# A two-layer decoder on one core: TensorE's order in the hybrid attention loop, ScalarE's copies there, and filler products in the head

## The chip, the core and the metric

The kernel runs on one core of a Trainium2 chip. A core has five engines that take their instructions in order and wait for each other on semaphores: TensorE (PE) multiplies matrices out of the on-chip memory into eight banks of result memory (`PS[:, 0..7, :]`), VectorE (DVE) and ScalarE (ACT) read and write both memories, GpSimd (POOL) works on the on-chip memory alone, and SyncE (SP) starts transfers. The metric is the device time of the whole program in microseconds (us), the median of three runs.

## What is computed

Eight sequences of 256 tokens with 256 features pass through six residual blocks, each on the layer-normalised state. Cut to what matters:

```python
x = x + mixer(ln(x))                       # low-rank state mixer, folded into one 256x256 matrix
x = x + cross_attention(ln(x), ctx, mask)  # one head, 64 context tokens, masked
x = x + bit_ffn(ln(x))                     # ternary weights, activations rounded to 8 bits, biases
x = x + self_attention(ln(x))              # 16 heads of 16, causal
x = x + hybrid_attention(ln(x), ctx)       # 16 query heads, 4 key heads of 128, RMS norm and rotary
                                           # turn on queries and keys; keys are 64 context tokens
                                           # plus the causal 256 tokens
x = x + top1_experts(ln(x))                # router of 32 experts, masked ternary weights

def hybrid(x, ctx):                        # the block that most of the change is in
    q = rope(rms(x @ wq) * qw); k = rope(rms(x @ wk) * kw); k_ctx = rms(ctx @ wk_ctx) * kw
    p = softmax(q @ concat(k_ctx, k).T / sqrt(128) + causal)
    return (p @ concat(ctx @ wv_ctx, x @ wv)) @ wo
```

## The kernel before

The stages follow each other: a head (mixer and cross attention of all batches, and the rounding of the feed-forward weights) up to about 82 us of the profiled span, the feed-forward block to about 190 us, self attention to about 435 us, the hybrid block from there to about 1093 us, and the routed experts. Every engine has its own program, written out by hand, and the order in it is the order on the chip.

**The hybrid loop** (`hybrid` in each engine's program) runs over 8 batches; batches 0 to 2 are written out, 3 to 6 come from a loop over pairs, and 7 is written out. Each batch has 8 iterations i, one for each half of the tokens (j = i // 4) and each key head (g = i % 4) with its 4 query heads. u = 8b + i counts them. One iteration works on several u at once. TensorE, in order:

- `scores(u+1, (0, 1))`: two of the four score tiles, into banks 3 and 4, out of `eQT`, the turned query;
- one odd piece of work (`values`, `xt_turn`, `keys`, `route`, `turn_keys`), which with few exceptions writes bank 2;
- `raw_query(u+3)`: four 512-wide passes into bank 1;
- `outputs(u-2)`: the turned probabilities `ePT` times the values, into bank 0;
- more odd pieces (`values(b, par, 1)` at i = 0, `keys` 0 and 1 at i = 1 and 2), `hybrid_out` (32 passes with `wo`, bank 2) at i = 4 for the batch before and at i = 7 for this one;
- `scores(u+1, (2, 3))`;
- `turn_query(u+2)`: the finished query `eQA` is turned into bank 2;
- `turn_probs(u-1)`: 5 turned tiles for the first half of the tokens (j = 0), 9 for the second, into banks 5, 6 and 7.

ScalarE copies bank 2 to `eQT` (`turned_query`, L1682), takes the squares of the raw query (`query_squares`, L1675), the exponentials (`exps`, L1691), the full turned tiles of bank 5 (`turned_probs`, L1698) and the output (`outputs`, L1705), and empties bank 2 for the odd pieces (`raw_keys` L1617 and L1618, `turned_keys` L1626 to L1631, `values` L1711 to L1714). VectorE masks scores and takes their maxima (`masked_max`, L847), turns the query by its angle (`rotate_query`, L817 and L823) and finishes it (`finish_query`, L829 and L833), normalises (L856, L859), and copies the rest of the turned tiles (`turned_probs`, L866 to L868; L866 is the full tile in bank 6, for j = 1 only). For the next batch's keys it has `square_key` (L734) and `turn_key` (L745 to L759). At i = 7 come `token_stats` (L881, L885), `choose` (L906 to L917) and `hybrid_finish` (L873), which adds the block's output to the tokens and frees bank 2. GpSimd computes the scales (`query_scales`, `key_squares`, `key_scales`).

What sets the order at one place is a single line on TensorE: `scores(u+1, ...)` begins with `pe.wait_ge(e_qc, v + 1)`, ScalarE's copy of the turned query, and between `turn_query` and that wait only `turn_probs` stands.

**The head** (`head(n)`, n = 0 to 8) does mixer work for batch n+1 and cross attention for batch n. On ScalarE six calls of `magnitude` (L1502) sum the weights, which then gives the scale `rgam`; `rounding` (L1508) rounds six pieces; VectorE clips them and makes the rows of biases (`bias_rows`, L460 to L467: a chain of eight instructions at n = 4). All matrix helpers go through `product` at L1842, so TensorE's rows carry that line; tiles tell them apart: `wq` is `raw_query`, `arena` into `EW`, `w_in` or `w_out` is `outputs`, `wk` is `keys`, `EW` with `arena` is `scores`.

## Time and profile before

| | us |
|---|---|
| median of 3 runs | 1186.63 (1184.10 to 1187.51) |
| the profiled execution | 1187.17 |
| its span in the trace | 1184.3 |
| TensorE busy | 1041.7 (88%) |
| VectorE busy | 877.1 (74%) |
| ScalarE busy | 653.8 (55%) |
| GpSimd busy | 326.3 (28%) |

TensorE's busy time counts a modelled end for each pass, so short waits are partly hidden in it; the distance from one start to the next is the safer reading. Its granted clock has two levels, 2.4 GHz (1.00 in the rows) and 1.2 GHz. In a timeline, "x4" joins four passes (two 32-bit products), and the bracket gives idle time before the first one with what ended it.

### The profile page before, as it was taken

Reading aid. Unit: us, or ns where it says so; the run is one execution under the profiler, and the core shown is the slowest. Engines: PE = TensorE matmul, PEld = TensorE weight load, DVE = VectorE, ACT = ScalarE, POOL = GpSimd, SP = SyncE. Lnnn points to the kernel's source line nnn. Section 1 sums busy time; section 2 is a strip of 40 time slices with the busy share of each in tenths; the row PEclk is TensorE's granted clock in tenths of the full one; section 3 lists DMA queues with packets and bytes.
Section 4 is the critical chain, followed back from the end, with each engine's and each line's share of the span. In section 5 each row is a group of like instructions: output and inputs, shape, how many; then the busy total and the mean of one; then the engine's idle time right before and its main releaser. Section 6 shows DMA issues by size and latency. Waiting matters only on the chain.

```text
span 1184.3 us, 21508 instructions
## 1 busy us (share of the span) xinstructions
PE 1041.7 (88%) x6293; PEld 716.7 (61%) x6301; DVE 877.1 (74%) x2458; ACT 653.8 (55%) x2010; POOL 326.3 (28%) x528
## 2 busy tenths in 40 slices
PE   7788886898999957899999999999999999988395
PEld 5654445676666634565766756657666666666385
DVE  5777774778877767877877878878878788764285
ACT  2777783655555524556556565565565645741262
POOL 3342222111111321312323223223232232101465
PEclk7979997999999978899999999999999999999598
DMA  9710001111111004000000000000000000000731
GB/s 286 251 35 2 1 1 54 55 55 54 53 53 53 19 1 133 26 1 14 1 14 1 1 14 1 5 10 1 16 1 0 14 1 0 15 1 24 263 99 45
DMA packets 38875, 49.58 MB, mean 42 GB/s; under 512 B 5110, under 2 KB 29564, under 8 KB 38528
## 3 DMA queue, kind: packets, MB, share of 16 engines
q1 hardware_dynamic: 36160, 44.16, 12.4%
q0 software_dynamic: 2304, 4.24, 1.0%
q8 instruction: 35, 0.57, 0.2%
q14 instruction: 56, 0.46, 0.1%
q10 hardware_dynamic: 320, 0.15, 0.1%
HBM read 32.70 MB, written 14.78 MB: 40 GB/s over the span
## 4 chain that ended last, share of the span: by engine, by line
PE 47%; ACT 4%; issue 4%; POOL 4%; DVE 3%; DMA 0%; DVEq 0%; ACTq 0%; POOLq 0%
PE PS L1842 41%; POOL out_dram L1417 3%; PE PS L2229 2%; PE PS L2209 2%; ACT arena L1682 1%; POOL tokens_dram L1393 1%; PE PS L2086 1%; DVE arena L823 1%; ACT arena L1691 1%; DVE arena L859 0%; DVE arena L847 0%; ACT early L1618 0%; PE PS L2231 0%; PE PS L2274 0%; PE PS L1852 0%
## 5 line engine op out<-in xcount | busy, mean ns | idle before, releaser
L1842 PE MATMUL PS<-early,arena 128*32 128x128 f32 (+6 forms) x920 | 122.2, 361 | 46.0 <-DVE early L713 23.7
L1842 PE MATMUL PS<-EW,arena 128*128 128x256 f32 (+7 forms) x512 | 121.2, 360 | 16.8 <-DVE small L847 7.3
L1842 PE MATMUL PS<-wq,EW 128*128 128x512 f32 x256 | 125.7, 614 | 6.8 <-DVE arena L823 6.6
L1331 POOL TENSOR_SCALAR small<-small 128x4 f32<-128x4 f32 x64 | 18.6, 291 | 385.2 <-ACT mask L1675 215.5
L1842 PEld LDWEIGHTS PS<-early,arena 128*32 128x32 f32 (+4 forms) x928 | 62.4, 121 | 99.8 <-issue 38.0
L847 DVE CUSTOM_DVE_ANT_0 arena<-PS,kmask 128x128 f32<-128x128 f32 (+3 forms) x256 | 91.4, 389 | 41.4 <-PE PS L1842 35.9
L1691 ACT ACTIVATE arena<-arena,small 128x128 f32<-128x128 f32 (+3 forms) x256 | 119.5, 473 | 0.5 <-DVE small L852 0.3
L1842 PE MATMUL PS<-wo,early 128*128 128x256 f32 x512 | 115.0, 384 | 3.6 <-DVE sinT L900 2.8
L1842 PEld LDWEIGHTS PS<-EW,arena 128*128 128x128 f32 x512 | 83.5, 193 | 43.7 <-issue 23.0
L1842 PEld LDWEIGHTS PS<-wo,early 128*128 128x128 f32 x512 | 98.6, 193 | 17.7 <-DVE sinT L900 3.2
L1682 ACT ACTIVATE arena<-PS 128x512 f32<-128x512 f32 x64 | 38.2, 597 | 114.5 <-PE PS L2209 114.1
L781 DVE TENSOR_REDUCE small<-PS 128x4 f32<-128x512 f32 x64 | 58.2, 951 | 43.1 <-PE PS L1842 43.1
L1675 ACT ACTIVATE mask<-PS 128x128 f32<-128x128 f32 x256 | 66.6, 275 | 41.0 <-PE PS L1842 40.8
L1842 PEld LDWEIGHTS PS<-wq,EW 128*128 128x128 f32 x256 | 45.4, 192 | 50.4 <-issue 42.2
L1333 POOL TENSOR_TENSOR small<-small,halves 128x4 f32<-128x4 f32 x64 | 69.1, 1079 | 5.4
L859 DVE TENSOR_SCALAR arena<-arena,small 128x128 f32<-128x128 f32 (+3 forms) x256 | 68.8, 333 | 2.3
L1611 ACT ACTIVATE early<-PS 128x384 f32<-128x384 f32 x64 | 28.6, 488 | 72.3 <-PE PS L2113 72.2
L1842 PE MATMUL PS<-arena,EW 128*128 128x512 f32 (+1 forms) x160 | 63.4, 510 | 2.6 <-ACT arena L1698 2.1
L1656 ACT ACTIVATE arena<-PS,small 128x256 f32<-128x256 f32 x128 | 63.1, 493 | 0.0
L1655 ACT ACTIVATE arena<-PS,small 128x128 f32<-128x128 f32 x128 | 48.8, 381 | 25.1 <-DVE small L781 24.5
L1217 POOL TENSOR_SCALAR ve<-mv 128x2 f32<-128x2 f32 x23 | 5.1, 223 | 190.9 <-DVE mv L416 190.3
L2113 PE MATMUL PS<-ident,arena 128*128 128x128 f32 x384 | 55.5, 279 | 0.4 <-ACT early L1611 0.4
(343 smaller groups left out, 2435.7 us busy)
## 6 DMA issues: line engine op xcount, KB each, us to landing
EW<-in_masksT_dram SPq DMA_DIRECT2D x32, 256.0 KB, 3.5
tokens_dram<-EW SPq DMA_DIRECT2D x1, 4160.0 KB, 16.1
arena<-tokens_dram SPq DMA_DIRECT2D x16, 260.0 KB, 2.8
results_dram<-EW SPq DMA_DIRECT2D x32, 128.0 KB, 3.2
EW<-results_dram SPq DMA_DIRECT2D x4, 1024.0 KB, 10.5
X<-in_x_dram SPq DMA_DIRECT2D x8, 256.0 KB, 5.1
wq<-in_wq_dram SPq DMA_DIRECT2D x1, 2048.0 KB, 11.1
wo<-in_wo_dram SPq DMA_DIRECT2D x1, 2048.0 KB, 18.5
```

Of the source, the lines that this page charges most:

```text
L781: last = dve.tensor_reduce(d_neg[:, i % 2, j, :], PS[:, 0:4, at:at + n], AX.X, ALU.max, negate=True)
L847: dve.tensor_tensor_reduce(probs(i, t), PS[:, 3 + t % 2, 0:n], kmask[:, at:at + n], 1.0, LOWEST, ALU.add, ALU.max, e_max[:, t:t + 1]).then ...
L859: last = dve.tensor_scalar(probs(i, t), probs(i, t), e_inv[:, t:t + 1], None, ALU.mult)
L1333: pool.tensor_tensor(e_rqs[:, i % 2, :], e_q3[:, i % 2, :], halves[:, 0:GH], ALU.pow).then_inc(e_rq, 1)
L1417: pool.indirect_dma_start(out_rows[:, :], bass.IndirectOffsetOnAxis(ap=to, axis=0), sY[:, k, t, :], None, bounds_check=B * S - 1, oob_is_e ...
L1655: act.activation(dP[:, i % 2, r, 0:P], PS[:, r, 0:P], ACT.Exp, bias=d_neg[:, i % 2, 0, r:r + 1])
L1656: act.activation(dP[:, i % 2, r, P:3 * P], PS[:, r, P:3 * P], ACT.Exp, bias=d_neg[:, i % 2, 1, r:r + 1]).then_inc(d_e, 1)
L1675: last = act.activation(eSQ[:, h * XD:(h + 1) * XD], PS[:, 1, h * XD:(h + 1) * XD], ACT.Square, accum_out=e_q2[:, i % 2, h:h + 1])
L1682: act.activation(eQT.rearrange("p (t h q) -> p h t q", t=4, h=GH), PS[:, 2, :].rearrange("p (h t q) -> p h t q", t=4, h=GH), ACT.Copy).the ...
L1691: last = act.activation(tile, tile, ACT.Exp, bias=e_neg[:, i % 2, t:t + 1], accum_out=e_sum[:, i % 2, t:t + 1])
L1842: return pe.matmul(dst, lhs, rhs, start=first, stop=last)
L2113: last = pe.transpose(PS[:, 4 + r % 2, k * P:(k + 1) * P], dP[:, i % 2, r, k * P:(k + 1) * P], ident[:, :])
```

## The change

In the **hybrid loop**, TensorE: `turn_query(u+2)` now stands ahead of `outputs(u-2)`. `keys` 0, 1 and 2 are made at i = 1, 3 and 4, ahead of `raw_query` (before: 0 and 1 at i = 1 and 2, behind `outputs`, and 2 at i = 3). `values(b, par, 1)` goes to bank 7 instead of bank 2. `hybrid_out` stands ahead of `outputs` too. ScalarE: `exps` moves ahead of the evictions of bank 2, `turned_query` ahead of `outputs`, and `turned_probs` also copies bank 6 where j = 1, which VectorE's L866 did. VectorE's `square_key` moves from i = 2, 3, 4 to i = 2, 4, 7, and GpSimd's key work follows the new times.

In the **head**: of the bias rows' chain, four of the scalings and copies move to ScalarE (`bias_round`, at n = 4, 5, 6; biasB's last scaling among them) and two combining steps stay on VectorE, spread over n = 5 and 6. `rounding` is spread, one piece at a time, over the starts and ends of n = 4 to 7. `cross_normalise` stands ahead of the computation of `gam`. TensorE gets `keep_going`: products of ones whose result nobody reads, 8 ahead of the wait for `c_fold`, 3 ahead of `folds`, 4 at each n from 4 to 8 (10 at n = 7), and twice 4 in `head_end`.

```diff
+            def bias_round(k):
+                act.wait_ge(s_c, mark["unit"] if k == 0 else mark[f"rest{k - 1}"])
...
@@ ScalarE, hybrid
-            def turned_probs(v):
+            def turned_probs(v, i):
                 act.wait_ge(e_t, v + 1)
                 after(act, e_pv, v)
-                act.activation(ePT[:, 0:512], PS[:, 5, :], ACT.Copy).then_inc(e_pta, 1)
+                for k in range(1 + i // XG):
+                    last = act.activation(ePT[:, 512 * k:512 * k + 512], PS[:, 5 + k, :], ACT.Copy)
+                last.then_inc(e_pta, 1)
...
-                        turned_probs(u - 2)
+                        turned_probs(u - 2, (i - 2) % 8)
+                    exps(u, i)
...
-                    exps(u, i)
                     if further[3]:
                         query_squares(u + 3, (i + 3) % 8)
+                    if i == 0:
+                        values(b, par, 1)
                     if i == 7 and routed:
                         weights(b - 2)
+                    if further[2]:
+                        turned_query(u + 2)
                     if i >= 2:
                         outputs(b, i - 2)
@@ VectorE, hybrid
-                if i >= XG:
-                    dve.tensor_copy(ePT[:, 512:1024], PS[:, 6, :])
...
-                    if 2 <= i <= 4 and nxt[0] == HYBRID:
-                        square_key(nxt[1], i - 2)
+                    if i in (2, 4, 7) and nxt[0] == HYBRID:
+                        square_key(nxt[1], {2: 0, 4: 1, 7: 2}[i])
@@ TensorE, head and hybrid
+            def keep_going(n, at=6):
+                for _ in range(n):
+                    product(PS[:, at, 0:P], ones[:, :], ones[:, :])
...
+                if n >= 4:
+                    keep_going(10 if n == B - 1 else 4, 4)
...
-                    if i == 3 and more:
-                        keys(nxt[1], 1 - par, 2)
+                    if i in (1, 3, 4) and more:
+                        keys(nxt[1], 1 - par, {1: 0, 3: 1, 4: 2}[i])
...
                         raw_query(u + 3, (i + 3) % 8, pars[3])
-                    if i >= 2:
-                        outputs(u - 2, i - 2, par)
...
                     if i == 0:
-                        pe.wait_ge(e_vr, 2 * b + 1)
-                        values(b, par, 1)
+                        after(pe, e_ptd, u - 1)
+                        values(b, par, 1, 7)
...
                         turn_query(u + 2, (i + 2) % 8)
+                    if i >= 2:
+                        outputs(u - 2, i - 2, par)
```

TensorE's order at i = 3 of a batch in the loop over pairs, before (`wk` is `keys`, `wq` the raw query, `arena` into `w_in` and `EW` the outputs, `EW` into `arena` the scores, L2209 the turn of the query, L2229 the turned probabilities):

```order
L1842 MATMUL PS<-wk,EW 128x512 x2
L283 REGISTER_ALU
L1842 MATMUL PS<-wq,EW 128x512 x2
L1842 MATMUL PS<-arena,w_in 128x512
L1842 MATMUL PS<-arena,EW 128x256
L283 REGISTER_ALU
L1842 MATMUL PS<-EW,arena 128x288
L283 REGISTER_ALU
L1842 MATMUL PS<-EW,arena 128x320
L2353 REGISTER_ALU
L2209 MATMUL PS<-ident,arena 128x128 x4
L2229 MATMUL PS<-ident,arena 128x128 x4
```

and in the change (L2231 and L2251 are the same two turns):

```order
L1854 MATMUL PS<-wk,EW 128x512 x2
L283 REGISTER_ALU
L1854 MATMUL PS<-wq,EW 128x512 x2
L283 REGISTER_ALU
L1854 MATMUL PS<-EW,arena 128x288
L283 REGISTER_ALU
L1854 MATMUL PS<-EW,arena 128x320
L2361 REGISTER_ALU
L2231 MATMUL PS<-ident,arena 128x128 x4
L1854 MATMUL PS<-arena,w_in 128x512
L1854 MATMUL PS<-arena,EW 128x256
```

The outputs moved from in front of the scores to a place behind the turn of the query.

TensorE's order at i = 7, before (`wo` is `hybrid_out`):

```order
L1842 MATMUL PS<-wq,EW 128x512 x2
L1842 MATMUL PS<-arena,EW 128x512 x2
L1842 MATMUL PS<-arena,w_out 128x256
L1842 MATMUL PS<-wo,early 128x256 x16
L283 REGISTER_ALU
L1842 MATMUL PS<-EW,arena 128x160
L283 REGISTER_ALU
L1842 MATMUL PS<-EW,arena 128x192
L2209 MATMUL PS<-ident,arena 128x128 x4
L2229 MATMUL PS<-ident,arena 128x128 x8
L2231 MATMUL PS<-ident,arena 128x128
```

and in the change:

```order
L1854 MATMUL PS<-wq,EW 128x512 x2
L1854 MATMUL PS<-wo,early 128x256 x16
L283 REGISTER_ALU
L1854 MATMUL PS<-EW,arena 128x160
L283 REGISTER_ALU
L1854 MATMUL PS<-EW,arena 128x192
L2231 MATMUL PS<-ident,arena 128x128 x4
L1854 MATMUL PS<-arena,EW 128x512 x2
L1854 MATMUL PS<-arena,w_out 128x256
L2251 MATMUL PS<-ident,arena 128x128 x8
L2253 MATMUL PS<-ident,arena 128x128
```

`hybrid_out` follows the raw query at once, and the outputs follow the turn of the query.

ScalarE's order at i = 6, before (L1698 turned probabilities, L1626 to L1631 turned keys, L1691 exponentials, L1675 squares):

```order
L1698 ACTIVATE arena<-PS 128x512
L1626 ACTIVATE EW<-PS 128x4x128
L1628 ACTIVATE EW<-PS 128x4x64
L1631 ACTIVATE EW<-PS 128x4x128
L1691 ACTIVATE arena,small<-arena,small 128x256 x2
L1691 ACTIVATE arena,small<-arena,small 128x320 x2
L1671 REGISTER_ALU
L1675 ACTIVATE mask,small<-PS 128x128 x4
```

and in the change (L1713 turned probabilities, L1705 exponentials, L1640 to L1645 turned keys, L1689 squares):

```order
L1713 ACTIVATE arena<-PS 128x512 x2
L1705 ACTIVATE arena,small<-arena,small 128x256 x2
L1705 ACTIVATE arena,small<-arena,small 128x320 x2
L1640 ACTIVATE EW<-PS 128x4x128
L1642 ACTIVATE EW<-PS 128x4x64
L1645 ACTIVATE EW<-PS 128x4x128
L1685 REGISTER_ALU
L1689 ACTIVATE mask,small<-PS 128x128 x4
```

The exponentials moved ahead of the turned keys, and there are two copies of turned tiles instead of one.

## Rows read from the trace of the kernel before

**Rows 1.** Busy us of PE, PEld, DVE, ACT, POOL over 50 us; clock; DMA; GB/s

```profile
750.00:800.00 50.00, 48.32 (x207) 30.86 (x205) 38.26 (x134) 29.70 (x113) 11.91 (x23) 1.00 0.04 9
```

**Rows 2.** TensorE's timeline, one hybrid batch: start us, us, engine, line, operation, [idle before]

```profile
751.26 1.98 PE L1842 MATMUL PS<-wq,EW 128*128 128x512 f32 x4 [0.46 <-DVE arena L823]
...
755.23 7.07 PE L1842 MATMUL PS<-wo,early 128*128 128x256 f32 x32
...
781.64 0.86 PE L1842 MATMUL PS<-EW,arena 128*128 128x160 f32 x4
783.01 0.66 PE L2209 MATMUL PS<-ident,arena 128*128 128x128 f32 x4 [0.50 <-ACT early L1618]
...
785.49 1.88 PE L1842 MATMUL PS<-wq,EW 128*128 128x512 f32 x4
787.21 1.02 PE L1842 MATMUL PS<-arena,w_in 128*128 128x512 f32 x2
...
788.50 1.88 PE L1842 MATMUL PS<-wk,EW 128*128 128x512 f32 x4
...
790.65 0.76 PE L1842 MATMUL PS<-EW,arena 128*128 128x160 f32 x4
791.25 0.60 PE L2209 MATMUL PS<-ident,arena 128*128 128x128 f32 x4
...
792.13 0.27 PE L2231 MATMUL PS<-ident,arena 128*128 128x128 f32 x1
792.70 1.07 PE L1842 MATMUL PS<-EW,arena 128*128 128x224 f32 x4 [0.30 <-ACT arena L1682]
...
829.64 0.71 PE L1842 MATMUL PS<-EW,arena 128*128 128x96 f32 x4
830.80 1.55 PE L1842 MATMUL PS<-wq,EW 128*128 128x512 f32 x3 [0.46 <-DVE arena L823]
```

**Rows 3.** ScalarE's timeline in the same batch

```profile
791.97 0.60 ACT L1682 ACTIVATE arena<-PS 128x512 f32<-128x512 f32 x1 [0.88 <-PE PS L2209]
...
823.50 0.60 ACT L1626 ACTIVATE EW<-PS 128x512 f32<-128x512 f32 x1 [0.77 <-PE PS L2086]
...
824.74 0.52 ACT L1691 ACTIVATE arena<-arena,small 128x256 f32<-128x256 f32 x1
...
826.81 0.27 ACT L1675 ACTIVATE mask<-PS 128x128 f32<-128x128 f32 x1
```

**Rows 4.** VectorE's timeline in the same batch

```profile
755.41 0.69 DVE L747 TENSOR_TENSOR early<-early,cosk 128x512 f32<-128x512 f32 x1
...
762.45 0.42 DVE L873 TENSOR_TENSOR X<-X,PS 128x256 f32 x1 [1.66 <-PE PS L1842]
...
822.95 0.68 DVE L866 COPY arena<-PS 128x512 f32<-128x512 f32 x1
...
825.57 0.69 DVE L833 TENSOR_TENSOR arena<-arena,small 128x512 f32<-128x512 f32 x1
```

**Rows 5.** TensorE's timeline, first batch of the hybrid loop

```profile
496.49 1.94 PE L1842 MATMUL PS<-EW,arena 128*128 128x224 f32 x4 [3.76 <-DVE small L847]
...
498.97 3.78 PE L1842 MATMUL PS<-wq,EW 128*128 128x512 f32 x4
```

**Rows 6.** TensorE's timeline in the head

```profile
13.92 3.75 PE L1842 MATMUL PS<-early,arena 128*128 128x256 f32 x8 [0.78 <-DVE early L534]
```

**Rows 7.** VectorE's timeline in the head

```profile
51.59 0.48 DVE L462 TENSOR_SCALAR early<-early,small 128x512 f32<-128x512 f32 x1
...
55.12 0.69 DVE L541 TENSOR_TENSOR X<-X,PS 128x512 f32<-128x512 f32 x1
```

**Rows 8.** ScalarE's timeline in the head

```profile
25.88 1.05 ACT L1502 ACTIVATE arena<-EW 128x1024 f32<-128x1024 f32 x1
```

**Rows 9.** SyncE's transfers, first 60 us: issue of the third weight

```profile
10.46 0.60 SPq L1132 DMA_DIRECT2D EW<-in_outT_dram  x1
```

**Rows 10.** Transfers by line, first 60 us: KB each, median us to landing

```profile
EW<-in_outT_dram SPq DMA_DIRECT2D x1, 1024.0 KB, 14.9
```

125 lines of the change are left out of this document (65 added, 60 removed).

## The prediction

> **What bounds the kernel now.** I first read the busy times of 50 us stretches: from 500 to 1050 us, the hybrid loop, TensorE is busy about 97% at full clock, VectorE 77% and ScalarE 59% [rows 1]. So there only what TensorE does not spend on its own passes can be won. I then read its timeline from start to start. One batch lasts 830.80 - 751.26 = 79.54 us [rows 2]. Its passes back to back: a raw query 787.21 - 785.49 = 1.72, outputs 788.50 - 787.21 = 1.29 for j = 0 and, with two more 512-wide passes, 2.15 for j = 1; second pair of scores 791.25 - 790.65 = 0.60 for j = 0, and by its columns 1.02 for j = 1; `hybrid_out`, 32 passes, 7.07 less the usual 0.17 of overlap = 6.90 [rows 2]. Summed: 8 raw queries 13.8, outputs 13.8, 3 `keys` and 2 `values` 8.7, `hybrid_out` twice 13.8, scores 12.3 (the first pairs at 0.54 and 0.91), query turns 3.5, probability turns 6.1 (0.55 and 0.98), the other turns and routing 2.9: 74.9 us. So **4.6 us of a batch are waits**, and that is the most that the reordering can return per batch.
>
> Where they are [rows 2]: after the last turned tile at 792.13, the scores start at 792.70; 0.11 of the 0.57 is the tile itself, 0.46 a wait for ScalarE's copy of the turned query. It comes where only 5 tiles are turned in between (i = 1 to 4), so 1.84 a batch. At 781.64 to 783.01 the scores take 1.37 instead of 0.60: 0.77 for the eviction of the context keys. At 829.64 to 830.80 the raw query waits 0.6 for VectorE. The other 1.4 are pieces under 0.35.
>
> **The hybrid part, step by step.** A turned query needs from the turn's start 791.25 to ScalarE's start at 791.97 [rows 3] 0.72, then 0.60 and 0.13 until scores start: 1.45 (792.70 - 791.25). Now outputs and turned tiles lie in between: 0.44 + 1.29 + 0.55 = 2.28 in the shortest iteration. The 1.84 goes, with 0.8 to spare if ScalarE is there in time. It is: its squares take 1.0 and begin when the raw query ends, 0.6 + 0.72 before the copy is due.
>
> `keys` ahead of `raw_query` give the eviction 1.72 + 0.60 of cover, so the 0.77 goes, although `exps` (826.81 - 824.74 = 2.07 for j = 1, 1.65 for j = 0) [rows 3] now stand before it: counted from the iteration's start, at i = 1 ScalarE ends its token norm at 0.9, two copies at 2.0, `exps` 3.6, `raw_keys` 4.6; TensorE asks at 0.54 + 1.86 + 1.72 + 0.60 = 4.7. Cover is exactly used up. At i = 2 the turned input is evicted at 3.2 to 3.3, asked for at 3.3. `values(b, par, 1)` in bank 7 drops one wait of 0.25.
>
> VectorE loses a 0.68 copy four times a batch [rows 4], and its rotation of the query no longer waits behind scores that come after outputs. The wait at 830.80 goes.
>
> **Waits that the change makes.** At i = 6 ScalarE has, from the start: two copies to 1.15, `exps` to 3.2, three copies of turned keys 824.74 - 823.50 = 1.24 [rows 3] to 4.45; TensorE is ready to write bank 2 after 0.91 + 0.43 + 1.72 + 1.02 = 4.1. Wait **0.5**. At i = 7 `hybrid_out` begins 2.15 + 0.6 earlier, but what frees bank 2 is `hybrid_finish`, at the end of VectorE's queue. Before, VectorE's L747 to the end of `choose` ran from 755.41 to 762.45 - 1.66 = 760.79, and it was 1.66 early [rows 4]. After: `exps` end at 3.2 of the iteration, normalising 4.65, `square_key` (new here, 0.6) 5.25, the 5.4 us block 10.65, `hybrid_finish` 11.1. TensorE asks at 0.54 + 1.72 + 6.90 + 0.60 = 9.76. Wait **1.4**. With 0.1 elsewhere the new waits are 2.0, so a batch gains 4.6 - 2.0 = **2.6**, and the new period is 76.9.
>
> By batch: 2 to 6 gain 5 x 2.6 = 13.0. Batch 1 routes nothing, `choose` is missing and the 1.4 with most of its cause: 3.8. Batch 0 has no `outputs` to cover VectorE's key turns at i = 4; TensorE idled 3.76 there and then ran a raw query at half clock, 3.78 against 1.88 [rows 2, 5]. `square_key` moved away, and the scores come earlier, but VectorE's chain (four copies and masks, 2.0; query 1.4; normalising after `exps` at 4.7; then 0.6, 1.3 and 2.7) ends at 9.3 where TensorE asks at 7.65: 1.7 to 2.1 idle remain. With the waits of its other iterations, 6.5; with the clock kept, 9; without, 4. Batch 7 has no next batch; its routing now waits behind `exps`: 1.0 (-1 to 3). **Hybrid: 24.3.**
>
> A rule of the Trainium skill speaks against the copies' move: "ScalarE: Activation LUTs", section "Rules for kernel authors", wants plain elementwise work on VectorE and budgets about 0.3 us plus 0.83 ns per element for an ACTIVATE, an estimate of 0.72 for 512. Here the copy lasts 0.60 on ScalarE and 0.68 on VectorE [rows 3, 4], so the trace disagrees. By the page the wait at i = 6 would grow from 0.5 to 0.9 and the sum shrink by some 3 us.
>
> **The head.** The mixer's 8 passes at 13.92 take 3.75 at half clock [rows 6]; at full clock they would take about 1.9. The 8 fillers fit before `c_fold` and could save 1.8 here and 1.0 just before. But ScalarE's first `magnitude` starts at 25.88 [rows 8] and needs the third weight, issued at 10.46 and 14.9 under way [rows 9, 10]: landed at 25.4. So no more than about 0.5 passes that point on ScalarE; what TensorE gains in being early may add 1. At n = 4 VectorE's bias chain, 55.12 - 51.59 = 3.53 [rows 7], holds the next mixer's addition; it goes, and 1.5 comes back at n = 5 and 6. ScalarE gets four passes of 0.5 and is next in the chain, so I take 1.5 of it. Fillers after n = 4 cost 34 x 0.21 = 7 us of TensorE at full clock if they were all on the path, less what a kept clock returns. Bounds -5 to +7; I take **3.0**, nearest to the bias chain less the ScalarE work. The feed-forward and self-attention stages and the tail are untouched.
>
> **Sum:** 24.3 + 3.0 = 27.3 off the profiled 1187.17: 1159.9. The median lies 0.5 below that execution, but the terms are no finer: **1160**.
>
> **Rivals.** (a) *ScalarE late.* It now begins each iteration behind a copy of outputs that come last on TensorE. The cover at i = 1, 2, 5, 6 was 0 to 0.8; if each copy comes 0.6 later than I have it, four waits of 0.6 take 2.4 of the 2.6, and 7 batches give back 16: 1176. For it: the zeros of cover above. Against: ScalarE is idle 0.88 before the copy at 791.97 [rows 3].
>
> (b) *VectorE late: slower.* `finish_query` had 3.3 us of slack behind outputs; now the turn of the query asks 3.3 after the start at i = 2 and 4.1 at i = 5, 6. Before, from the copy at 822.95 to the multiply's end at 826.26 were 3.3 [rows 4], 2.7 without the copy. That decides: if the rotation ends more than 0.6 after the iteration's start, as it did in this row (1.0), each such iteration waits. With 1.25 at i = 2, 3, 5, 6, a batch pays 5.0 + 2.0 against 4.6, +2.4, and 7 batches +17; without the head's gain 1203. Against: squares end 1.2 and rotation 2.6 after the raw query, the next iteration starts after 2.9.
>
> (c) *The head pays.* Fillers stand in the path at half clock: +6, so 1169.
>
> (d) *Nearly all waits go.* The block at i = 7 is shorter than I count and batch 0 keeps its clock: 2 us more in six batches, 2.5 in batch 0, 3 in the head: 1146.
>
> **Chances.** Forecast (1153 to 1167) 0.50; (a) or part of it, 1167 to 1181, 0.20; (c) 0.08; (d) 0.12; (b) 0.06; no gain because (a) and (c) join, 0.04. The range 1148 to 1178 leaves out (b), half of (d) and the ends of (a). Measurement tells 0.3%, 3.6 us, from nothing: faster 0.90, same 0.04, slower 0.06.
>
> **What would show it.** Right: a batch period of 77 us; no wait of the scores on the turned query's copy; a turn of the query that waits about 1.4 for VectorE's addition at i = 7 and about 0.5 for ScalarE's turned keys at i = 6; about 2 us idle at i = 4 of batch 0; the first 82 us shorter by about 3. Wrong: waits of the query's turn on VectorE's multiply at i = 2, 5 or 6 (b), or a head that ends later than before.

## The result, and the profile after

The changed kernel takes 1175.87 us, median of 5 runs (1173.85 to 1176.54); beside it the kernel before takes 1186.58 us, median of 5 (1182.61 to 1187.51). The ratio is 0.9915, with a 95% interval of 0.9894 to 0.9935: faster, by 10.7 us. The forecast was 27 us, so the sign and the range held and the size did not. Three later comparisons, each on one chip, gave ratios of 0.9899, 0.9895 and 0.9905.

The profiled execution after has a span of 1174.1 us (before: 1184.3). The difference of 10.2 us is split up in one table, read off TensorE's timeline: the moments at which the `values` product of each batch begins, and VectorE's last `hybrid_finish`.

| us | before | after | gain | forecast |
|---|---|---|---|---|
| start of the first `values` product (end of head, feed-forward and self-attention) | 453.19 | 453.34 | -0.2 | 3.0 |
| batch 0 | 75.51 | 70.03 | 5.5 | 6.5 |
| batch 1 | 78.10 | 74.51 | 3.6 | 3.8 |
| batches 2 to 6, each | 78.68 to 79.78 | 77.33 to 77.56 | 9.4 in all | 13.0 |
| batch 7, to the start of the last `hybrid_finish` | 89.27 | 96.06 | **-6.8** | 1.0 |
| from there to the end | 91.5 | 92.8 | -1.3 | 0 |

The middle of the loop is what was foreseen. Busy time of PE, PEld, DVE, ACT and POOL in the stretch of [rows 1], with clock, DMA share and GB/s: TensorE went from 48.32 to 49.97 of 50 us. The stretch lies between two of the new waits, so it looks better than the batch as a whole.

```profile
750.00:800.00 50.00, 49.97 (x225) 33.33 (x224) 37.88 (x127) 31.28 (x115) 13.17 (x19) 1.00 0.04 9
```

TensorE's timeline of the same batch after the change, to be held against [rows 2] (start us, us, engine, line, operation, idle before):

```profile
784.19 0.27 PE L2253 MATMUL PS<-ident,arena 128*128 128x128 f32 x1
784.29 0.98 PE L1854 MATMUL PS<-EW,arena 128*128 128x224 f32 x4
...
811.12 0.66 PE L2231 MATMUL PS<-ident,arena 128*128 128x128 f32 x4 [0.48 <-ACT EW L1645]
...
823.82 0.76 PE L1854 MATMUL PS<-EW,arena 128*128 128x160 f32 x4
826.16 0.66 PE L2231 MATMUL PS<-ident,arena 128*128 128x128 f32 x4 [1.58 <-DVE X L870]
```

The scores at 784.29 start 0.10 after the turned tile at 784.19; before, they came 0.57 after it. The waits on the turned query and on the keys are gone. Two new ones stand where they were expected: 0.48 for ScalarE's turned keys at iteration 6, and at iteration 7 the scores take 2.34 us to the next start (826.16 - 823.82) instead of 0.60, so 1.74 go to waiting for VectorE's addition in `hybrid_finish` (L870).

The surprise is the last batch. TensorE's timeline at iterations 6 and 7, first in the kernel before, then in the changed one:

```profile
1054.75 0.60 PE L2274 MATMUL PS<-ident,causal 128*128 128x128 f32 x4
1055.19 1.88 PE L1842 MATMUL PS<-arena,EW 128*128 128x512 f32 x4
...
1057.34 0.97 PE L1842 MATMUL PS<-rwT,XT 128*128 128x32 f32 x8
...
1066.29 8.85 PE L1842 MATMUL PS<-wo,early 128*128 128x256 f32 x32 [2.78 <-DVE sinT L900]
```

```profile
1036.96 1.08 PE L1854 MATMUL PS<-rwT,XT 128*128 128x32 f32 x8 [2.79 <-ACT XT L1745]
...
1038.98 3.53 PE L1854 MATMUL PS<-arena,EW 128*128 128x512 f32 x4
...
1050.33 10.02 PE L1854 MATMUL PS<-wo,early 128*128 128x256 f32 x32 [6.36 <-DVE sinT L897]
```

Before, after turning the tokens (L2274) TensorE ran `outputs` and came to `route` (the `rwT` product) when ScalarE had copied the turned tokens. After, it waits 2.79 us for that copy (L1745), and the `outputs` that follow run at half clock (3.53 instead of 1.88). Then, ahead of `hybrid_out`, it waits 6.36 us for VectorE's copy of the logits (L897) instead of 2.78, and the output product takes 10.02 us instead of 8.85 (6.9 is its length at full clock). ScalarE's timeline says why `route` is late:

```profile
1034.26 0.51 ACT L1705 ACTIVATE arena<-arena,small 128x256 f32<-128x256 f32 x1
...
1036.33 0.58 ACT L1745 ACTIVATE XT<-PS 128x512 f32<-128x512 f32 x1
```

The copy stands behind the 2.07 us of `exps` (L1705), which the change put ahead of it.

### The profile page after: what moved, and what is told of

Its sections match the earlier page's. It is cut to its first block, busy times and chain, and to the rows that moved or that the text cites. A ratio compares the mean times of both kernels' runs of the same rounds, so it can differ in the third digit from the quotient of the medians.

```text
span 1174.1 us, 21695 instructions
## 1 busy us (share of the span) xinstructions
PE 1032.6 (88%) x6383; PEld 719.0 (61%) x6383; DVE 850.6 (72%) x2422; ACT 669.1 (57%) x2046; POOL 319.8 (27%) x528
## 4 chain that ended last, share of the span: by engine, by line
PE 40%; issue 6%; ACT 5%; POOL 4%; DVE 2%; SPq 1%; DMA 0%; DVEq 0%; POOLq 0%; ACTq 0%
PE PS L1854 33%; PE PS L2251 3%; POOL out_dram L1415 3%; PE PS L2231 3%; ACT arena L1705 2%; ACT arena L1713 1%; POOL small L1323 1%; PE PS L2253 1%; PE PS L2108 1%; SPq L1189 1%; DVE small L878 0%; ACT mask L1689 0%; ACT EW L1645 0%; ACT EW L1640 0%; DVE X L870 0%
## 5 line engine op out<-in xcount | busy, mean ns | idle before, releaser
L1854 PE MATMUL PS<-early,arena 128*32 128x256 f32 (+6 forms) x928 | 118.2, 353 | 45.5 <-DVE early L712 23.7
L1854 PE MATMUL PS<-EW,arena 128*128 128x256 f32 (+7 forms) x512 | 115.6, 349 | 11.3 <-DVE small L846 8.4
L1854 PE MATMUL PS<-wq,EW 128*128 128x512 f32 x256 | 123.2, 604 | 1.5 <-DVE arena L822 1.5
L1705 ACT ACTIVATE arena<-arena,small 128x128 f32<-128x128 f32 (+3 forms) x256 | 119.5, 475 | 4.1 <-DVE small L851 4.1
L1854 PEld LDWEIGHTS PS<-early,arena 128*32 128x32 f32 (+4 forms) x928 | 59.6, 118 | 98.0 <-issue 34.5
L1689 ACT ACTIVATE mask<-PS 128x128 f32<-128x128 f32 x256 | 67.1, 281 | 47.6 <-PE PS L1854 47.3
L1696 ACT ACTIVATE arena<-PS 128x512 f32<-128x512 f32 x64 | 38.9, 608 | 85.4 <-PE PS L2231 85.4
L1721 ACT ACTIVATE early<-PS 128x512 f32<-128x512 f32 x64 | 38.2, 597 | 84.7 <-PE PS L1854 84.7
L1713 ACT ACTIVATE arena<-PS 128x512 f32<-128x512 f32 x96 | 53.9, 596 | 13.9 <-PE PS L2253 11.7
```

Of the source, the lines that this page charges most:

```text
L1689: last = act.activation(eSQ[:, h * XD:(h + 1) * XD], PS[:, 1, h * XD:(h + 1) * XD], ACT.Square, accum_out=e_q2[:, i % 2, h:h + 1])
L1696: act.activation(eQT.rearrange("p (t h q) -> p h t q", t=4, h=GH), PS[:, 2, :].rearrange("p (h t q) -> p h t q", t=4, h=GH), ACT.Copy).the ...
L1705: last = act.activation(tile, tile, ACT.Exp, bias=e_neg[:, i % 2, t:t + 1], accum_out=e_sum[:, i % 2, t:t + 1])
L1713: last = act.activation(ePT[:, 512 * k:512 * k + 512], PS[:, 5 + k, :], ACT.Copy)
L1721: act.activation(eOT[:, GH * g:GH * g + GH, j * P:(j + 1) * P].rearrange("p h (t q) -> p h t q", t=4), PS[:, 0, :].rearrange("p (t h q) -> ...
L1854: return pe.matmul(dst, lhs, rhs, start=first, stop=last)
```

## The experiments

All kernels are named by what differs from the changed kernel. Times are compared within one group, since groups ran on different chips (the kernel before had medians of 1184.8 to 1188.9 us there). The changed kernel itself ran again in three of the five groups. It did not run in that of the token copy, the two outputs, the addition and the first run of the old head; there the ratio to the kernel before is the measure (0.9895 to 0.9915 for the changed kernel elsewhere). The stage durations of all profiles stand in the table at the end of this section.

**The last batch: the token copy ahead of the exps.** ScalarE, `hybrid`:

```diff
                     if i >= 2 or former:
                         turned_probs(u - 2, (i - 2) % 8)
+                    if i == 6 and not more:
+                        token_copy(b - 1, 2)
                     exps(u, i)
...
-                    if i == 6 and not more:
-                        token_copy(b - 1, 2)
```

> The changed kernel with one thing put back: in the last cross-attention batch, at iteration 6, ScalarE copies the turned tokens (token_copy) ahead of the exps of that iteration, as in the kernel before. The span of the changed kernel lost 6.8 us between the first values product and the last hybrid_finish of the last batch (96.06 us against 89.27 before). Theory 1 (this one copy behind the exps delays route, the logits and the output product, and lets the clock fall): the wait of 2.79 us ahead of route falls below 1, the wait of 6.36 us ahead of the last output product falls to about 3, the last batch comes to 91 or less, and the time is 3 to 6 us under the 1175.9 of the changed kernel: about 1171. Rival (the other moves in that batch, ScalarE's two copies of turned probabilities or the outputs behind the long output product, hold it): the last batch stays above 94, the time is within 1.5 us of 1175.9.

Measured 1166.99 us (ratio to before 0.9852, 0.9818 to 0.9887). The last batch took 92.5 us. TensorE's timeline:

```profile
1031.32 1.08 PE L1854 MATMUL PS<-rwT,XT 128*128 128x32 f32 x8 [0.74 <-ACT XT L1745]
...
1033.34 1.88 PE L1854 MATMUL PS<-arena,EW 128*128 128x512 f32 x4
...
1042.99 10.21 PE L1854 MATMUL PS<-wo,early 128*128 128x256 f32 x32 [6.36 <-DVE sinT L897]
```

The wait for `route` falls from 2.79 to 0.74 and the outputs behind it run at full clock (1.88). But the wait of 6.36 has not moved at all: half of the theory falls. The copied logits (L897) come behind VectorE's `normalise` and `choose` of iteration 7, and these behind the exps and the turned probabilities of that iteration, which follow TensorE's own turns (L2253). That chain is as long as before. What changed is what TensorE does meanwhile.

**And the two outputs ahead of the output product.** As above, with TensorE's order in the last two iterations of the last batch put back:

```diff
+                    if i >= 6 and not more:
+                        outputs(u - 2, i - 2, par)
                     if i == 6 and not more:
                         route(b - 1, 2)
...
-                    if i >= 2:
+                    if 2 <= i < (8 if more else 6):
                         outputs(u - 2, i - 2, par)
-                    elif former:
+                    elif i < 2 and former:
```

> As last_copy, and in iterations 6 and 7 of the last batch TensorE's outputs stand ahead of route and of the long output product, as in the kernel before. Theory 1 (the copy alone holds the loss): within 1 us of last_copy, about 1171. Rival (the output product ahead of the two outputs holds the other half, since the outputs ran while TensorE would have waited for the logits): 2 to 4 us below last_copy, 1168 to 1169, and the last batch at 88 to 89 us.

Measured 1167.04 us (0.9838, 0.9808 to 0.9869), the same median as with the copy alone; the last batch took 90.1 us.

```profile
1043.32 0.59 PE L1854 MATMUL PS<-arena,w_out 128*128 128x256 f32 x2
1046.68 8.86 PE L1854 MATMUL PS<-wo,early 128*128 128x256 f32 x32 [2.77 <-DVE sinT L897]
```

Now the outputs fill the chain: 2.77 us of waiting are left, as before the change (2.78), and the output product takes 8.86 us instead of 10.21, also as before the change (8.85). The last batch in twelve profiles of unchanged code there lies between 93.6 and 97.7 us, mean 95.6. So the copy alone (92.5) is 1.1 below the lowest of them, and both together (90.1) 3.6 below, within 0.8 of the kernel before. So these two moves hold the loss, 6.8 us in the first pair of profiles. How it divides between them is known only roughly: by stage durations 3 and 2.4, from one profile each, while the medians of the two kernels are equal; the start of the loop scatters by more than the second.

**VectorE's addition ahead of the token statistics.**

```diff
                         if nxt[0] == HYBRID:
                             turn_key(nxt[1], 2)
+                        if nxt[0] == HYBRID:
+                            hybrid_finish(b, 0)
                         if former and nxt[0] == HYBRID:
                             token_stats(b - 1)
                         if routed:
                             choose(b - 2)
                         if nxt[0] == HYBRID:
-                            hybrid_finish(b, 0)
                             if routed:
```

> The changed kernel with one thing moved: at iteration 7 of every batch but the last, VectorE's hybrid_finish (eight rows of the output product into the residual) stands ahead of token_stats and choose instead of behind them. The trace shows TensorE waiting 1.6 to 1.7 us per batch there, ahead of turning the query. Theory 2 (that wait is real and nothing takes its place): 1.4 to 1.7 us for each of 7 batches, 10 to 12 us off: 1164 to 1166. Rival (normalise and rotate of the next iterations are late instead, so that ScalarE's or VectorE's chain gives the wait back at the next scores): less than 4 us off, 1172 or more.

Measured 1165.85 us (0.9828, 0.9797 to 0.9860). The steady period falls from 77.5 to 75.8 us: 1.4 to 1.7 for each batch from 2 to 6, and 0 and 0.1 for batches 0 and 1, which pay no such wait. VectorE's and TensorE's timelines at the end of iteration 7:

```profile
819.64 0.42 DVE L870 TENSOR_TENSOR X<-X,PS 128x256 f32 x1 [0.81 <-PE PS L1855]
```

```profile
819.44 0.76 PE L1855 MATMUL PS<-EW,arena 128*128 128x160 f32 x4
820.12 0.66 PE L2232 MATMUL PS<-ident,arena 128*128 128x128 f32 x4
```

VectorE now waits for TensorE (0.81) and TensorE no longer for VectorE: the turn of the query follows the scores in 0.68. The wait was real, and nothing took its place. That the time is the expected one is in part luck: the 10 to 12 us off counted seven batches; five pay the wait, and their stage durations give 7.9.

**ScalarE's turned keys ahead of its exps at iteration 6.**

```diff
+                    if i == 6 and more:
+                        turned_keys(nxt[1], 1 - par, 1)
                     exps(u, i)
...
-                    if i == 6 and more:
-                        turned_keys(nxt[1], 1 - par, 1)
```

> The changed kernel with one thing moved: at iteration 6 of every batch but the last, ScalarE's copy of the turned keys stands ahead of the exps instead of behind. TensorE waits 0.48 us there per batch. Theory (the wait is all that the order costs): it goes, 0.3 to 0.5 us a batch, 2 to 4 us in all, about 1173. Rival (the exps are then late, since the copy waits for TensorE to turn the keys, and the wait of the turned probabilities grows by as much or more): no gain, 1175 to 1179.

Measured 1169.92 us against 1172.35 of the changed kernel in that group (ratios 0.9877 and 0.9899, their intervals overlap); the period falls from 77.5 to 76.8. The 0.48 goes, a wait of 0.58 for VectorE's rotation comes in iteration 7, and the wait for the addition shrinks to 0.77, since TensorE arrives later at it. So one delay was moved and one merged:

```profile
814.60 1.98 PE L1854 MATMUL PS<-wq,EW 128*128 128x512 f32 x4 [0.58 <-DVE arena L822]
...
824.86 0.66 PE L2231 MATMUL PS<-ident,arena 128*128 128x128 f32 x4 [0.77 <-DVE X L870]
```

**The second full tile of turned probabilities on VectorE again.** This undoes one part of the change:

```diff
                 after(dve, e_pv, v)
+                if i >= XG:
+                    dve.tensor_copy(ePT[:, 512:1024], PS[:, 6, :])
...
-                for k in range(1 + i // XG):
-                    last = act.activation(ePT[:, 512 * k:512 * k + 512], PS[:, 5 + k, :], ACT.Copy)
-                last.then_inc(e_pta, 1)
+                act.activation(ePT[:, 0:512], PS[:, 5, :], ACT.Copy).then_inc(e_pta, 1)
```

> The changed kernel with one thing put back: VectorE again copies the second full tile of turned probabilities in iterations 4 to 7 (0.68 us each) instead of ScalarE (0.60). Theory (VectorE is the later engine at iterations 4 and 7, ScalarE only at 6): 0.5 to 1.5 us a batch slower, 1179 to 1186, since hybrid_finish and the masked maxima come later by 0.68. Rival (ScalarE is the later engine in most of the batch, and the copy that it took over costs more than it brings): 1170 to 1175.

Measured 1167.26 us (0.9856, 0.9824 to 0.9888) against 1172.35 (0.9899, 0.9871 to 0.9927). The intervals just overlap; the durations of the batches decide. The rival holds in its sign, the theory doesn't, and the time is below the range of both. The period is 76.5 instead of 77.5 us, without the wait at iteration 6 and with 1.15 instead of 1.6 to 1.7 at iteration 7:

```profile
815.92 0.76 PE L1854 MATMUL PS<-EW,arena 128*128 128x160 f32 x4
817.82 0.66 PE L2231 MATMUL PS<-ident,arena 128*128 128x128 f32 x4 [1.15 <-DVE X L872]
```

Although VectorE has 0.68 us more to do in that iteration, it ends sooner: its `normalise` waits for the exps, and these stood behind ScalarE's second copy. Both engines must be done before TensorE goes on, but in this order: ScalarE, then VectorE. Work moved from the second of a chain to the first lengthens the chain unless the second was busy in the meantime; here VectorE was waiting (0.71 us ahead of L855 in the changed kernel):

```profile
818.13 0.18 DVE L855 RECIPROCAL small<-small 128x4 f32<-128x4 f32 x1 [0.71 <-ACT arena L1705]
...
825.69 0.42 DVE L870 TENSOR_TENSOR X<-X,PS 128x256 f32 x1
```

The Trainium skill ("ScalarE: Activation LUTs", section "Rules for kernel authors") gives plain elementwise work to VectorE. For this copy the run agrees with its advice, though not with the reason, VectorE's speed per element: one copy lasts 0.60 us on ScalarE and 0.68 on VectorE, and the gain comes from which of the two is waited for. The budget that the prediction takes from the same section is for an ACTIVATE with its bias as a pointer operand, which this copy has not; the rows have 0.60.

**The first batch: masked maxima ahead of the turned keys.**

```diff
+                    if i == 4 and not former:
+                        masked_max(u + 1, (i + 1) % 8, (2, 3))
+                        rotate_query(u + 3, (i + 3) % 8)
                     if i == 4:
                         if nxt[0] == HYBRID:
                             turn_key(nxt[1], 0)
```

> The changed kernel with one thing moved: in the first cross-attention batch, at iteration 4, VectorE's masked_max of the later two heads and rotate stand ahead of the two turn_key of the next batch. The trace shows TensorE idle for 4.20 us there, ahead of the query product, and that product then at half clock (2.56 us instead of 1.88). Theory (those two masked maxima behind 14 key copies hold the whole idle): the idle falls below 1 us, the clock stays, the first batch's period falls from 74.5 to 69.5 to 71 and the time by 3.5 to 5. Rival (the turned keys come late for iteration 5 instead): the idle moves there, the period falls by less than 1.5 us.

Measured 1172.81 us against 1172.35 (0.9884 and 0.9899): no difference that the runs can tell. The first batch takes 68.2 us; in the eleven profiles of kernels that leave it as it is, 70.0 to 71.8. So 1.8 to 3.6 are gained there, less than expected, and the idle of 4.20 splits into 0.96, 1.39 and 0.41 instead of going. First the changed kernel, then this one:

```profile
492.80 1.81 PE L1854 MATMUL PS<-EW,arena 128*128 128x224 f32 x4 [4.20 <-DVE small L846]
...
495.15 2.56 PE L1854 MATMUL PS<-wq,EW 128*128 128x512 f32 x4
```

```profile
493.69 0.43 PE L2111 MATMUL PS<-ident,early 64*128 64x64 f32 x4 [0.96 <-issue]
494.05 1.98 PE L1857 MATMUL PS<-wq,EW 128*128 128x512 f32 x4
497.43 1.26 PE L1857 MATMUL PS<-EW,arena 128*128 128x288 f32 x4 [1.39 <-DVE small L846]
```

VectorE's own timeline tells why the idle was so long. Before the change, then after it, at the last step of turning the second key:

```profile
495.24 0.69 DVE L759 TENSOR_TENSOR early<-early,small 128x512 f32<-128x512 f32 x1
```

```profile
485.13 0.68 DVE L733 TENSOR_REDUCE small<-early 128x4 f32<-128x512 f32 x1
...
491.55 0.69 DVE L758 TENSOR_TENSOR early<-early,small 128x512 f32<-128x512 f32 x1 [2.43 <-POOL small L1323]
```

Before, VectorE went straight on. In the changed kernel it stands idle for 2.43 us, waiting for GpSimd's scale of that key: the change moved the key's sum of squares (`square_key`, here L733) from i = 3 to i = 4, directly ahead of the step that needs the scale, and GpSimd does its other work first. With the masked maxima and the rotation put in front, VectorE has that time filled. In the later batches the same wait of 2.4 to 2.7 us stands in VectorE's timeline, but TensorE has `hybrid_out` to do meanwhile. That the 2.43 is what lengthens TensorE's idle follows from the two timelines; no run moved `square_key` back.

**The head.** The changed loop with the head of the kernel before (no filler products, the bias rounded on VectorE):

> Head of the kernel before with the cross-attention part of the change. By the two traces the head gained nothing (the loop's first scores at 452.36 us against 452.20). Theory (the head is worth 0): 1175.5 to 1176.5, as the changed kernel. Rival (the head change did bring its 3 us and something in the first batch gives them back): 1178 to 1180. Rival (the fillers cost clock or time): 1172 to 1174.

> The head of the kernel before with the cross-attention part of the change, beside the changed kernel on the same chip. Theory (new head worth 1 to 3 us on the median): 1 to 3 above after_third. Rival (worth nothing): within 1 us.

> The head of the kernel before with the cross-attention part of the change, the measure for the next: about 2.5 us above after_fourth, one batch of about 79 us, ScalarE idle about 4 us ahead of the copies of turned probabilities at the start of batch 5.

This kernel ran in three groups: 1175.99 (ratio 0.9921), 1179.92 (0.9935; the changed kernel beside it 1177.40, 0.9895) and 1177.70 (0.9927; beside it 1175.29, 0.9905). So it looked as if the new head brought 2.4 to 2.5 us, though its profiles showed no earlier start of the loop. But all three of its profiles have one batch, number 5, of 79.1 to 79.6 us, where the changed kernel has 77.6. Batch 5 is the first after the loop over pairs of batches branches back. ScalarE's timeline there, and TensorE's:

```profile
835.99 1.08 ACT L1698 ACTIVATE arena<-PS 128x512 f32<-128x512 f32 x2 [4.50 <-issue]
```

```profile
839.84 0.66 PE L2206 MATMUL PS<-ident,arena 128*128 128x128 f32 x4 [1.81 <-ACT EW L1713]
```

ScalarE stands for 4.50 us with nothing that it waits for ("issue"), and TensorE then waits 1.81 for it. In the changed kernel the same gap is 2.1 to 2.2 and is hidden. Hence a kernel that puts only six one-column copies, of no use, at the start of ScalarE's program, so that its loop lies where it lies in the changed kernel:

```diff
             act.activation(h_table, ones[:, 0:1], ACT.Exp)
+            for k in range(509, 512):
+                act.activation(small[0:64, k:k + 1], ones[0:64, 0:1], ACT.Copy)
+                act.activation(small[64:128, k:k + 1], ones[64:128, 0:1], ACT.Copy)
```

> As hybrid_third, with six more one-column copies on ScalarE at the program's start (into columns that nothing reads, while its first inputs are still under way), so that its instructions of the loop stand at the places that they have in the changed kernel. Theory (at the loop's branch back ScalarE waits for its instructions, and how long depends on where they lie): its idle time there falls from 4.0 to 4.4 to 2.1 to 2.3, that batch from 79.1 or more to 77.6, and the time by 1.5 to 2. Rival (something that the old head leaves behind, or another engine's instructions, make it late): as hybrid_third within 1 us, with the 4 us idle.

Measured 1174.52 us (0.9902), batch 5 at 77.58 us, and the gap:

```profile
832.12 1.09 ACT L1701 ACTIVATE arena<-PS 128x512 f32<-128x512 f32 x2 [2.21 <-issue]
```

Six instructions more, 3.2 us less on the median (the intervals overlap), and 2.0 less in this one batch of the profile, where the three profiles without them agree. With that accident taken out, the old head (1174.5) is as fast as the new one (1175.3). The fillers alone:

```diff
-            keep_going(8)
...
-                if n >= 4:
-                    keep_going(10 if n == B - 1 else 4, 4)
...
-                keep_going(4, 4)
                 level_turn(0)
-                keep_going(4, 4)
...
-            keep_going(3)
```

> The changed kernel without the filler products of its head (the ten of the kernel before stay). Theory (they raise the clock between 55 and 80 us from 0.72 to 0.84 up to 0.86 to 0.93, but the chain through ScalarE's and VectorE's copies sets the end there): within 1 us of after_fourth. Rival (they are what the new head brings): 2 to 4 us slower than after_fourth. Rival (they stand in the path): 1 to 3 us faster.

Measured 1172.22 us (0.9887, 0.9855 to 0.9918) against 1175.29 (0.9905, 0.9873 to 0.9937): not slower, perhaps 3 us faster. Busy times and clock of two stretches of the head, first the kernel before, then the changed one, then the changed one without fillers:

```profile
0.00:55.00 55.00, 42.83 (x192) 31.48 (x192) 36.36 (x126) 25.66 (x59) 17.48 (x60) 0.84 0.91 289
55.00:80.00 25.00, 19.50 (x77) 14.86 (x78) 20.41 (x64) 17.56 (x37) 12.69 (x32) 0.72 0.00 1
```

```profile
0.00:55.00 55.00, 44.86 (x213) 34.32 (x213) 35.16 (x126) 24.36 (x57) 18.04 (x62) 0.84 0.92 289
55.00:80.00 25.00, 20.13 (x124) 16.84 (x123) 18.62 (x56) 21.24 (x43) 7.86 (x24) 0.93 0.01 2
```

```profile
55.00:80.00 25.00, 18.61 (x80) 13.85 (x80) 18.08 (x53) 18.63 (x39) 10.35 (x28) 0.79 0.00 1
```

From 55 to 80 us the fillers do raise the granted clock (0.72 to 0.84 in the eight profiles without them, 0.86 to 0.95 in the twelve with them), and bring nothing: the loop starts at 452.2 and 447.0 without them and at 447.1 to 455.7 with them. In the first 55 us the clock is 0.84 in one execution of the changed kernel and 0.94 in another, and the start of the loop scatters by 8.6 us over twelve profiles of the new head (mean 452.1) and by 5.0 over six of the old one (mean 452.3). A difference of 1 us in the head can't be seen through that.

Within the head it can. Take the distance between two of VectorE's additions to the tokens, over n = 4 and over n = 5. VectorE's timeline, first before, then in the changed kernel:

```profile
46.70 0.69 DVE L547 TENSOR_TENSOR X<-X,PS 128x512 f32<-128x512 f32 x1
...
56.80 0.66 DVE L547 TENSOR_TENSOR X<-X,PS 128x512 f32<-128x512 f32 x1
...
61.58 0.68 DVE L541 TENSOR_TENSOR X<-X,PS 128x512 f32<-128x512 f32 x1
```

```profile
48.49 0.69 DVE L545 TENSOR_TENSOR X<-X,PS 128x512 f32<-128x512 f32 x1
...
52.78 0.69 DVE L539 TENSOR_TENSOR X<-X,PS 128x512 f32<-128x512 f32 x1
...
54.80 0.69 DVE L545 TENSOR_TENSOR X<-X,PS 128x512 f32<-128x512 f32 x1 [0.26 <-PE PS L1854]
...
59.93 0.17 DVE L560 RECIPROCAL small<-small 128x2 f32<-128x2 f32 x1 [2.54 <-ACT arena L1525]
...
63.45 0.68 DVE L539 TENSOR_TENSOR X<-X,PS 128x512 f32<-128x512 f32 x1
```

Over n = 4, from 46.70 to 55.12 [rows 7] before and from 48.49 to 52.78 after, 8.42 us become 4.29: the bias chain is gone and gives 4.1. Over n = 5, 4.78 become 8.65: 3.9 are paid back at once. VectorE waits 2.54 us there for ScalarE's exponentials (L1525), which now stand behind the first bias step and two of the spread pieces of `rounding`. All six profiles of the old head have 8.4 and 4.8, all twelve of the new one with fillers 4.3 and 8.6 to 8.7, and the two without fillers 4.3 and 8.0; so 0.6 of the second is theirs.

**All that gained, together.** The last batch's two moves, the addition first, the copy back on VectorE, and the first batch's masked maxima:

> The changed kernel with what each gained in the runs before: hybrid_finish ahead of token_stats and choose (the steady batch's period was 75.8 with it), VectorE copying the second full tile again (76.5), the first batch's masked maxima ahead of the turned keys (1.8 off that batch), token_copy and the two outputs of the last batch in the order of the kernel before (6.0 off that batch). Theory (each takes away a wait of its own, and TensorE then hardly waits): steady period 75.2 to 75.5, that is 2.1 to 2.4 below 77.5; 14 for batches 1 to 6, 1.8 for the first, 6 for the last: 20 to 22 under the changed kernel, 1150 to 1154, ratio to before 0.970 to 0.974. Rival (two of them take away the same wait, and a third engine's chain holds the batch at 75.8): 1156 to 1160.

Measured 1153.89 us against 1177.40 of the changed kernel in its group: ratio to before 0.9703 (0.9675 to 0.9732). The steady period is 75.2 us, and TensorE's timeline of iterations 6 and 7 there has no wait above 0.2 us left:

```profile
800.63 0.66 PE L2235 MATMUL PS<-ident,arena 128*128 128x128 f32 x4
...
806.42 7.07 PE L1858 MATMUL PS<-wo,early 128*128 128x256 f32 x32
813.33 0.76 PE L1858 MATMUL PS<-EW,arena 128*128 128x160 f32 x4
814.01 0.66 PE L2235 MATMUL PS<-ident,arena 128*128 128x128 f32 x4
```

The gains add up to 23.5 us on the medians, where 20 to 22 were expected, but not from the terms expected: against the changed kernel's profile of that group, batches 1 to 6 give 10.9 (14 expected), the first 3.2 (1.8) and the last 9.1 (6). The sum is in part luck. The last batch takes 86.9 us, less than either kernel; with the copy on VectorE, for one thing, the waits of 1.18 for ScalarE's turned probabilities are back at 0.69.

Batch 5 stays about 1 us above its neighbours, at 76.1 to 76.4, in all four profiles of combined kernels. VectorE stands idle there after the branch back, and TensorE waits for it:

```profile
821.06 0.69 DVE L865 COPY arena<-PS 128x512 f32<-128x512 f32 x1 [2.06 <-issue]
```

```profile
822.30 1.98 PE L1858 MATMUL PS<-wv,EW 128*128 128x512 f32 x4 [0.62 <-DVE arena L867]
```

So what the branch back costs the engines is hidden in the changed kernel and comes out in these, where TensorE has hardly any other wait.

> As combined, with the head of the kernel before (no filler products, VectorE rounding the bias). Theory (the profiled pair showed the same start of the cross-attention loop with both heads, 453.3 and 453.2; but seven further profiles of the new head show it at 447.1 to 455.7, by the clock granted in the first 55 us, 0.84 to 0.94): the new head is worth 1 to 3 us on the median, so this is 1 to 3 above combined. Rival (worth nothing): within 1 us of it.

1153.87 us (0.9711): with this loop the two heads are equal. ScalarE's gap at the branch back is 2.17 us in both; that the program is shorter without the second copy, and so lies well with either head, is a reading that no run tests.

> The combined version without the filler products of the head. Theory (they cost about what no_fillers showed): 2 to 4 us below combined_again, about 1151. Rival (their cost was scatter of the head between executions, which spread the start of the cross-attention loop over 447 to 456 us): within 1.5 us of combined_again.

1148.93 us (0.9692, 0.9669 to 0.9715), against 1150.98 (0.9706, 0.9678 to 0.9733) of the combined version beside it. Twice, then, the kernel without fillers has the lower median, by 3.1 and 2.1 us, and twice the intervals overlap: the fillers gain nothing, and whether they cost 2 us stays open. This version is the fastest of all, 3.1% under the kernel before.

For the comparisons, the changed kernel and the combined one ran again unchanged.

> The changed kernel as it is, beside the others of this group on one chip, as their measure: 1175 to 1176, by both theories.

> The changed kernel as it is, the measure for the other three: 1172 to 1176, ratio to before 0.989 to 0.992; the start of the cross-attention loop in its profile goes with the clock granted in the first 55 us: at 0.94 about 447 to 452, at 0.84 about 453 to 456.

> The changed kernel as it is, the measure for the other three: ratio to before 0.989 to 0.992.

> The combined version as before, the measure for the other on the same chip: 1151 to 1155, ratio to before 0.968 to 0.973, the steady batch at 75.2.

Stage durations in the profiles, us (loop start; batches 0, 1, 4, 5; batch 7 to the start of the last `hybrid_finish`):

| kernel | start | 0 | 1 | 4 | 5 | 7 |
|---|---|---|---|---|---|---|
| before | 453.2 | 75.5 | 78.1 | 79.4 | 79.8 | 89.3 |
| after, four profiles | 447.1 to 453.5 | 70.0 to 71.2 | 74.5 | 77.5 | 77.6 | 93.6 to 97.1 |
| token copy first | 449.8 | 70.0 | 74.5 | 77.5 | 77.6 | 92.5 |
| and outputs first | 453.5 | 70.4 | 74.5 | 77.5 | 77.6 | 90.1 |
| addition first | 452.3 | 70.0 | 74.4 | 75.8 | 76.2 | 97.5 |
| keys first | 453.7 | 70.5 | 74.4 | 76.8 | 76.9 | 93.7 |
| copy on VectorE | 447.9 | 70.9 | 73.9 | 76.5 | 77.0 | 95.8 |
| maxima first | 455.7 | 68.2 | 74.5 | 77.5 | 77.6 | 93.7 |
| old head, three | 449.8 to 454.8 | 70.1 to 71.8 | 74.5 | 77.5 | 79.1 to 79.6 | 95.3 to 97.7 |
| old head, padded | 452.5 | 71.1 | 74.5 | 77.5 | 77.6 | 97.0 |
| no fillers | 452.2 | 70.4 | 74.5 | 77.5 | 77.6 | 93.7 |
| combined, two | 451.6, 455.2 | 66.8, 68.0 | 73.9 | 75.2 | 76.2 | 86.9, 85.3 |
| combined, old head | 450.0 | 67.9 | 73.9 | 75.2 | 76.4 | 87.2 |
| combined, no fillers | 447.0 | 67.9 | 73.9 | 75.2 | 76.1 | 85.3 |

## Why the prediction was right in its sign and wrong in its size

**Right.** TensorE's own passes bound the loop, and each wait named in [rows 2] went. The two waits that the change makes came at the iterations forecast, for the engines forecast: 0.5 against 0.48 at iteration 6, 1.4 against 1.74 at iteration 7. Rival (b) did not occur: no turn of the query waits long for VectorE's multiply. Batch 1 gave 3.6 for 3.8.

**Wrong 1, most of the miss: batch 7.** The step "Batch 7 has no next batch; its routing now waits behind `exps`: 1.0 (-1 to 3)" should have been about -6. It named `route` behind the exps without working out what that costs, and it didn't look at the outputs at all, which the change moves behind the output product. In the other batches that product waits for nothing; in the last it waits for the logits, and the trace of before showed it: TensorE waits 2.78 us there even with the outputs ahead. Work moved behind a wait that is already exposed no longer covers any of it: the wait grew from 2.78 to 6.36. Putting both orders back returned 3.6 to 7.6 us of that batch (against the twelve profiles), to within 0.8 of the kernel before.

**Wrong 2: the head, 3.0 against nothing.** The steps "what TensorE gains in being early may add 1" and "1.5 comes back at n = 5 and 6" failed. The bias chain's removal gave 4.1 us at n = 4, more than the 3.53 forecast, and 3.9 came back at n = 5 alone, because ScalarE's new pieces stand ahead of the exponentials that VectorE waits for. The clock rose where the fillers stand, but the start of the loop did not come earlier (453.34 against 453.19); with the padded old head the medians are 1174.5 and 1175.3. The bounds of -5 to +7 held it. Rival (c), that fillers stand in the path, is right in its mechanism and too large: 0.6 us at n = 5 is shown, 2 us in all may be, not 6.

**Wrong 3: the steady batch, 2.6 forecast, 1.9 measured.** The mechanism was right, three sizes were each off by 0.2 to 0.3: the mean of batches 2 to 6 was 79.35 before, not 79.54; without the waits it is 75.2, as far as the combined version shows, and not 74.9; and the waits after are 2.2 us and not 2.0. The better lesson lies in a term whose cost was not seen: the second copy on ScalarE was booked as relief of VectorE ("VectorE loses a 0.68 copy four times a batch"). It costs 1.0 us a batch, almost half of the new waits, since the exps stand behind it, and then VectorE. Rival (a) had waits for ScalarE at i = 1, 2, 5 and 6, 2.4 a batch; only the 0.48 at i = 6, which the forecast had itself, came, and the rest of the 1.0 through VectorE at i = 7. So ScalarE was late, but by another way and by less.

**Wrong 4: batch 0, 6.5 against 5.5.** At iteration 4, "1.7 to 2.1 idle remain" measured 4.20, more than the 3.76 of before [rows 5]. The step that failed is "`square_key` moved away": for the second key it moved to i = 4 itself, and the chain of VectorE's work was added up without a wait for GpSimd, which took 2.43. An estimate from these two rows: 4.20 - 2.43 = 1.77, what the forecast had. It was balanced in part by a product less slow (2.56 instead of 3.78).

The tail's 1.3 us is of the size of its scatter: from the end of the last addition it is 91.1 us before and 92.4 after, in fourteen other profiles 91.2 to 92.3, in four, all of one group, 94.8 to 95.4.

Sum of the misses: 7.8 in batch 7, 3.2 in the head, 3.6 in batches 2 to 6, 1.2 in batches 0 and 1, 1.3 in the tail: 17.1 of 27.3, which leaves the 10.2 of the two spans.

## What to carry to other kernels

When a loop is reordered for its steady state, read its last pass by itself: what covers a wait there may be just what the new order moves behind it, and the last pass can lose more (6.8 us here) than three steady ones gain (1.9 each). Before work goes from one engine to another, ask which of them the other waits for; a copy moved to the less busy engine made this chain longer, because the busier one was waiting for it. When work is moved next to the step that needs it, look at the third engine between the two, here GpSimd with its scale. And where two kernels differ by a few us in a loop, compare the passes one by one: a single pass that stands out, with the same work as its neighbours, can point to the program's placement.

## What the runs showed of the hardware

At the branch back of the loop over pairs of batches, ScalarE stands idle for 2.1 to 2.4 us with nothing to wait for in all kernels but one, and in that one for 4.0 to 4.5. The three profiles of that kernel (old head, new loop) agree, and six instructions more ahead of the loop bring the gap back to 2.21. In the changed kernel it is hidden at 2.2 us; with the old head at 4.5 TensorE waits 1.81 for it. VectorE has such a gap of 1.9 to 2.1 us there in all four profiles of combined kernels, and there TensorE waits 0.46 to 0.65 for it and the batch is about 1 us longer. That it is the fetching of instructions is a reading: the trace shows an instruction queue with a few transfers in that stretch, and no run here tells more of its rule than that the position of the loop in ScalarE's program matters.

The granted clock of the first 55 us differs between executions of the same code, from 0.84 to 0.94. In the changed kernel's four profiles the loop starts at 453.3 and 453.5 with 0.84, at 451.8 with 0.91 and at 447.1 with 0.94. That is no rule: with the same head the loop also starts at 452.3 with 0.94 (addition first), and in the combined kernel without fillers at 447.0 with 0.84.
